# A Macaron block on one core: score products that read 32 rows of the array, layer norms scaled on VectorE, keys stored once, a shorter lead-in

## What is computed

```python
x = x + 0.5 * ffn(layernorm(x))          # sum over 8 experts: (silu(x @ Wg) * (x @ Wu)) @ Wd, inner width 512
x = x + attention(layernorm(x))          # 16 heads of 8, rotary q and k, causal, relative positions clipped to 32
x = x + 0.5 * ffn(layernorm(x))          # the same weights

scores = einsum('bhqd,bhkd->bhqk', q, k) + einsum('bhqd,qkd->bhqk', q, rel)
attn   = softmax(where(causal, scores, -1e18))
ctx    = einsum('bhqk,bhkd->bhqd', attn, v) + einsum('bhqk,qkd->bhqd', attn, rel)
```

## Time and profile before

| | us |
|---|---|
| median of three runs | 1380.19 |
| lowest and highest run | 1377.62, 1382.7 |
| profiled execution, its time | 1373.76 |
| profiled execution, span from first to last instruction | 1371.8 |

### The profile page before, as it was taken

The page is one execution under the profiler, slowest core; times in us unless marked ns, Lnnn a source line. Parts: engine busy times, 40 slices in busy tenths (PEclk is TensorE's granted clock), DMA queues, the critical chain, the costliest instruction groups (busy, mean ns, idle before and its releaser), DMA issues. The chain is left out here.

```text
span 1371.8 us, 29322 instructions
## 1 busy us (share of the span) xinstructions
PE 1333.0 (97%) x8472; PEld 1074.1 (78%) x8472; DVE 1192.4 (87%) x2554; ACT 1105.2 (81%) x2642; POOL 1098.6 (80%) x1012
## 2 busy tenths in 40 slices
PE   8999999999999999999999999999999899999798
PEld 7878777777878788778878878777888788788586
DVE  6887988998999999889899989899989889999465
ACT  6765878888888889878888888888888788888354
POOL 7977879788888888877779877889888788878465
PEclk9999999999999999999999999999999999999899
DMA  5404799999999999999999999999999989998200
GB/s 184 158 1 136 137 226 173 183 215 161 196 200 179 182 182 188 208 160 181 172 190 207 180 178 170 178 215 183 175 184 172 204 165 179 177 182 147 45 1 8
DMA packets 719138, 225.07 MB, mean 164 GB/s; under 512 B 653057, under 2 KB 698497, under 8 KB 718977
## 3 DMA queue, kind: packets, MB, share of 16 engines
q1 hardware_dynamic: 562224, 180.84, 73.4%
q10 hardware_dynamic: 156752, 42.36, 17.0%
HBM read 60.95 MB, written 69.86 MB: 95 GB/s over the span
## 5 line engine op out<-in xcount | busy, mean ns | idle before, releaser
L1231 POOL TENSOR_TENSOR hid_lo<-hid,hid_hi 128x512 fp32r<-128x512 f32 x512 | 662.1, 1302 | 149.2 <-ACT hid_hi L932 116.4
L1079 DVE TENSOR_TENSOR hid<-hid,work 128x512 f32<-128x512 f32 x512 | 347.1, 680 | 63.1 <-PE work L729 59.2
L1073 DVE SCALAR_TENSOR_TENSOR hid<-hid,work 128x512 f32<-128x512 f32 x512 | 345.2, 679 | 32.0 <-ACT hid L926 31.0
L1246 POOL TENSOR_TENSOR probs<-exps,probs 128x512 f16<-128x512 f32 (+1 forms) x288 | 307.2, 1069 | 79.0 <-ACT probs L989 76.0
L932 ACT CAST hid_hi<-hid 128x512 fp32r<-128x512 f32 x512 | 318.1, 625 | 62.0 <-DVE hid L1079 46.3
L926 ACT ACTIVATE hid<-work 128x512 f32<-128x512 f32 x512 | 307.1, 602 | 73.1 <-PE work L729 52.7
L977 ACT ACTIVATE exps<-work,negmax_shifted 128x512 f32<-128x512 f32 (+2 forms) x320 | 193.0, 605 | 40.9 <-DVE negmax_shifted L1179 25.4
L1173 DVE TENSOR_REDUCE negmax<-work 128x1 f32<-128x384 f32 (+3 forms) x352 | 222.2, 633 | 1.8
L727 PE MATMUL work<-xt,wg 128*128 128x512 f32 x512 | 205.3, 401 | 3.4 <-DVE xt L1048 1.5
L810 PE MATMUL acc<-hid_lo,wd 128*128 128x512 f32 x512 | 205.8, 405 | 0.8 <-POOL hid_lo L1231 0.7
L727 PE MATMUL work<-xt,wu 128*128 128x512 f32 x512 | 204.2, 399 | 1.0 <-DVE hid L1073 0.4
(11 more groups left out here) (99 smaller groups left out, 1909.2 us busy)
## 6 DMA issues: line engine op xcount, KB each, us to landing
prob_window_scratch<-probs SPq DMA_DIRECT2D x384, 80.0 KB, 3.0
rel_win<-rel_window_scratch ACTq DMA_DIRECT2D x250, 96.0 KB, 3.5
q_scratch<-rope SPq DMA_DIRECT2D x16, 512.0 KB, 4.7
qq<-q_scratch ACTq DMA_DIRECT2D x32, 256.0 KB
k_scratch<-rope SPq DMA_DIRECT2D x16, 512.0 KB, 3.9
rel_window_scratch<-g_s SPq DMA_DIRECT2D x32, 256.0 KB, 3.0
k_pad<-k_scratch SPq DMA_DIRECT2D x128, 64.0 KB, 3.1
prob_window_scratch<-probs SPq DMA_DIRECT2D x32, 256.0 KB, 4.8
```

What stands on the lines that cost most here:

```text
L1073: dve.scalar_tensor_tensor(out=hid[:, arg % HB, :], in0=hid[:, arg % HB, :], scalar=1.0, in1=work[bank_of["gate", arg]][:, :], op0=ALU.add ...
L1079: dve.tensor_tensor(hid[:, arg % HB, :], hid[:, arg % HB, :], work[bank_of["up", arg]][:, :], ALU.mult).then_inc(s_hid, 1)
L1231: pool.tensor_tensor(hid_lo[:, arg % HH, :], hid[:, arg % HB, :], hid_hi[:, arg % HH, :].bitcast(F32), ALU.subtract).then_inc(s_hlo, 1)
L1246: pool.tensor_tensor(probs[:, arg % PB, cols:2 * cols], exp_of(arg)[:, 0:cols], probs[:, arg % PB, 0:cols], ALU.subtract).then_inc(s_plent, 1)
```

## The change

Four things change.

1. The `scores` of tiles 2 and 3 read only the 32 rows of `qq` and `k_pad` in which their head stands. The built program gives these 256 matmuls an array shape of 32 rows by 128 columns, at row 0, 32, 64 or 96; before, all `scores` had the shape 128 by 128. In the planner, the second task of a pair (`a` odd) takes 0.02 and is due at once, and the first takes 0.19 more than before.
2. `ln_scaled` moves from ScalarE to VectorE, as `(x - mean) * rstd`; GpSimd no longer makes `mean_neg` and `shift`.
3. k is stored in two copies, not four, and `load_k` reads each twice.
4. The lead-in has 14 transposes of the identity instead of 24. A pass's first `gate` multiplies with `x_hi` twice before it waits for `x_lo`, and the wait of `project_v` on the k store is out of the planner.

The due times (`LATER`, all numbers in it, and `UNITS_TO`) are others too.

```diff
-    UNITS_FROM, UNITS_TO = 146, 1406
+    UNITS_FROM, UNITS_TO = 146, 1394
...
-    LATER = {"acc": -121.4, "attention_sum": -318.4, "band_turn": -1036.1, "band_values": -446.9, "constants":
+    LATER = {"acc": -586.1, "attention_sum": -763.3, "band_turn": -795.8, "band_values": 49.4, "constants":
...
-        step("PE", 0.683, at, "gate", n, ("gated", back(n, 2)), split[0], *normed)
+        step("PE", 0.683, at, "gate", n, ("gated", back(n, 2)), split[0], *normed, ordered=rest)
...
-        step("POOL", 1.85, time, "ln_rstd", what, ("ln_stats", what))
-        step("ACT", 1.55, time, "ln_scaled", what, ("ln_rstd", what))
+        step("POOL", 1.3, time, "ln_rstd", what, ("ln_stats", what))
+        step("DVE", 0.75, time, "ln_scaled", what, ("ln_rstd", what))
...
-            step("PE", 0.02 + columns / 2286, due[k], "scores", k, ("load_q", quad // NT),
-                 ("load_k", quad // NT), done_with(back(k, 2)))
+            beside = HEADS[i] == 1 and a % 2 == 1
+            step("PE", 0.02 if beside else 0.02 + columns / 2286 + 0.19 * (HEADS[i] == 1), -1000 if beside else due[k],
+                 "scores", k, ("load_q", quad // NT), ("load_k", quad // NT), done_with(back(k, 2)))
...
-                    for copy in range(2):
-                        sp.dma_start(bass.AP((q_t, k_t)[i], base + copy * (1 + i) * P * L,
-                                             [[L, P], [(2 - i) * P * L, 2], [1, L]]),
-                                     rope[:, :, :]).then_inc(s_qst[i], 16)
+                    if i == 0:
+                        for copy in range(2):
+                            sp.dma_start(bass.AP(q_t, (t % VB * 4 + copy) * P * L, [[L, P], [2 * P * L, 2], [1, L]]),
+                                         rope[:, :, :]).then_inc(s_qst[0], 16)
+                    else:
+                        sp.dma_start(bass.AP(k_t, t % VB * 2 * P * L, [[L, P], [P * L, 2], [1, L]]),
+                                     rope[:, :, :]).then_inc(s_qst[1], 16)
...
-            for i in range(24):
+            for i in range(14):
                 done = pe.transpose(work[0][:, 0:P], ident[:, :], ident[:, :])
...
+                    pe.matmul(bank[:, :], wg[:, HI, e, cols], x_hi, start=True, stop=False)
+                    pe.matmul(bank[:, :], wg[:, LO, e, cols], x_hi, start=False, stop=False)
+                    if k == 0:
                         pe.wait_ge(s_xlo, LN["ln1" if kind == "A" else "ln3", t] + 1)
-                    bank = take_bank(name, arg)
-                    three(bank[:, :], wg[:, HI, e, cols], wg[:, LO, e, cols],
-                          x_hi, x_lo).then_inc(s_gate, 1)
+                    pe.matmul(bank[:, :], wg[:, HI, e, cols], x_lo, start=False, stop=True).then_inc(s_gate, 1)
...
-                    pe.matmul(bank[:, 0:len(places) * keys], qq[:, gg % 2, i * P:(i + 1) * P],
-                              k_pad[:, gg % 2, places[0]:places[-1] + 1, 0:keys],
+                    rows = slice(0, P) if len(places) > 1 else slice(R * places[0], R * places[0] + R)
+                    pe.matmul(bank[:, 0:len(places) * keys], qq[rows, gg % 2, i * P:(i + 1) * P],
+                              k_pad[rows, gg % 2, places[0]:places[-1] + 1, 0:keys],
                               start=True, stop=True).then_inc(s_sc, 1)
...
+            def norm_scaled(m, x, sums):
+                dve.wait_ge(s_rstd, m + 1)
+                wait(dve, s_xnt, m)
+                wait(dve, s_ftok, sums)
+                for i in range(NT):
+                    done = dve.tensor_scalar(xn[:, i * P:(i + 1) * P], x[:, i * P:(i + 1) * P], moments[:, i, 0:1],
+                                             rstd[:, i:i + 1], ALU.subtract, ALU.mult)
+                done.then_inc(s_xn, 1)
```

More of the change, by code:

```diff
@@ L103, in macaron_kernel @@
     LANDS = {"PE": 0.35, "ACT": 0.35, "DVE": 0.35, "POOL": 0.35, "SP": 2.6}
-    LATER = {"acc": -121.4, "attention_sum": -318.4, "band_turn": -1036.1, "band_values": -446.9, "constants":
-             -30.0, "down": 8.6, "down_lo": -201.5, "exp": 12.1, "fill": 1556.9, "gate": -44.0, "gated": 320.8, "hi": 3.0,
-             "largest": -216.4, "ln_hi": -7.5, "ln_lo": -70.0, "ln_rstd": 143.1, "ln_scaled": -27.0, "ln_stats": -82.5,
-             "ln_turned": -567.8, "lo": -140.6, "load_band": -538.1, "load_expert": -1404.6, "load_k": 925.9, "load_q":
-             8.6, "load_window": 12.9, "load_x": -367.9, "near": -197.6, "outproj": -318.4, "p_hi": -260.7, "p_lent":
-             -464.6, "p_lo": -295.1, "p_turn": -31.8, "prepare_hi": 633.1, "prepare_lo": -582.6, "product": 22.2,
-             "project": -628.0, "project_v": -251.4, "qk_hi": -662.7, "qk_lo": -982.2, "qk_store": -200.1, "qrel": 5.7,
-             "qrel_copy": -216.1, "qrel_store": -370.4, "recip": -1364.0, "recip_copy": -97.4, "recip_turned": -69.4,
-             "recip_wide": 306.1, "rotate": 670.1, "scale": -238.4, "scores": -342.4, "shift": -259.0, "split_hi": 409.2,
-             "split_lo": 142.9, "store": -956.4, "store_band": -1287.5, "sum": -1014.5, "sum_turned": -630.3, "tanh": -2.0,
-             "up": 0.9, "v_add": 219.3, "v_split": -42.6, "values": -864.8, "zero": 229.9}
@@ L119, in step @@
-    def step(engine, takes, time, name, arg, *after, lands=None):
-        before = ()
+    LATER = {"acc": -586.1, "attention_sum": -763.3, "band_turn": -795.8, "band_values": 49.4, "constants":
+             1562.7, "down": 36.2, "down_lo": 4.5, "exp": 22.5, "fill": 1007.1, "gate": 25.3, "gated": 41.8, "hi": 11.9,
+             "largest": -320.0, "ln_hi": -291.6, "ln_lo": -276.9, "ln_rstd": 547.2, "ln_scaled": 288.9, "ln_stats": -792.4,
+             "ln_turned": -33.9, "lo": -501.5, "load_band": -1429.9, "load_expert": -1522.6, "load_k": 106.2, "load_q":
+             -417.2, "load_window": 166.5, "load_x": -242.0, "near": 52.1, "outproj": -124.1, "p_hi": -556.7, "p_lent":
+             -546.4, "p_lo": -852.2, "p_turn": -27.3, "prepare_hi": 176.2, "prepare_lo": 600.1, "product": -245.7,
+             "project": -80.0, "project_v": 46.4, "qk_hi": -596.3, "qk_lo": -1272.1, "qk_store": 166.5, "qrel": 36.1,
+             "qrel_copy": -7.1, "qrel_store": -451.1, "recip": -864.4, "recip_copy": 134.5, "recip_turned": 31.0,
+             "recip_wide": 347.3, "rotate": 581.4, "scale": -677.2, "scores": 8.5, "shift": -492.5, "split_hi": -441.4,
+             "split_lo": -175.9, "store": 455.7, "store_band": -1215.8, "sum": -855.8, "sum_turned": -411.0, "tanh":
+             -408.2, "up": 26.9, "v_add": 419.0, "v_split": -263.7, "values": -273.2, "zero": 1378.1}
@@ L121, in step @@
+    def step(engine, takes, time, name, arg, *after, lands=None, ordered=()):
+        before = []
         if name in ("p_lo", "p_lent", "shift"):
@@ L127, in step @@
         steps[name, arg] = (engine, takes, LANDS[engine] if lands is None else lands, time + LATER.get(name, 0.0),
-                            [what for what in after if what[1] is not None], [what for what in before if what in steps])
+                            [what for what in after if what[1] is not None],
+                            [what for what in before if what in steps] + list(ordered))
     PARTS = {"split_hi": 3, "split_lo": 3, "project": 4, "rotate": 4, "qk_hi": 2, "qk_lo": 2, "qk_store": 2}
@@ L180, in macaron_kernel @@
         kind, t = PASSES[p]
-        normed = [("ln_lo", ("ln1" if kind == "A" else "ln3", t))] if k == 0 and p else []
+        normed = [("ln_hi", ("ln1" if kind == "A" else "ln3", t))] if k == 0 and p else []
+        rest = [("ln_lo", ("ln1" if kind == "A" else "ln3", t))] if k == 0 and p else []
         split = [("split_lo", (k // FC, piece)) if p == 0 and k % FC == 0 and k else ("", None) for piece in range(3)]
-        step("PE", 0.683, at, "gate", n, ("gated", back(n, 2)), split[0], *normed)
+        step("PE", 0.683, at, "gate", n, ("gated", back(n, 2)), split[0], *normed, ordered=rest)
         step("ACT", 0.488, at + 0.9, "tanh", n, ("gate", n), ("lo", back(n, HB)))
         step("DVE", wide(L), at + 1.5, "gated", n, ("tanh", n))
-        step("PE", 0.683, at + 1, "up", n, ("product", back(n, 2)), split[1], *normed)
+        step("PE", 0.683, at + 1, "up", n, ("product", back(n, 2)), split[1], *rest)
         step("DVE", wide(L), at + 2.3, "product", n, ("gated", n), ("up", n))
@@ L438, in macaron_kernel @@
         rstd = sb("rstd", [P, NT])
-        shift = sb("shift", [P, NT])
-        mean_neg = sb("mean_neg", [P, NT])
-        zeros = sb("zeros", [P, NT])
         minus_half = sb("minus_half", [P, NT])
```

37 lines of the change are left out of this document (12 added, 25 removed).

## The result

The changed kernel takes 1619.72 us (median of 4 runs, 1619.55 to 1619.89), the kernel before 1378.9 (median of 4, 1375.93 to 1382.7). The ratio is 1.1745, with a 95% interval of 1.1714 to 1.1776. The forecast was slower, by 61 us to 1441; it is slower by 241. The direction is right and the size is far off, well outside the range.

A forecast was written before the change was run, and what follows sets the result against it. The prediction took TensorE's stream of closely packed matmuls as the bound. It summed 79 - 2 - 6 - 10 = +61 us onto 1380.2, forecasting 1441 us, with an 8-in-10 range of 1362 to 1458.

The forecast's parts named there:

- the price of an excursion: TensorE: each switch to the 32-row shape and back loses 0.37 us (0.34 to 0.40).
- The term: TensorE's scores: 233 excursions cost 86 us, less 2.5 beside `values` and 4.6 for real pairs: +79 us.
- Waits close up, 10: TensorE's idle time, 20.0 us in the long stretch: half of it goes, 10 us gained.
- SP's queue loses eight issues: Key stores: eight of 16 go, loads stay hidden, cost nothing; up to 3 us could come back.
- the norm: Four VectorE operations at 0.21 us, 0.85 us per norm, 20 us over 24 norms, covered except at the two ends.
- the cover's loss: Norms on VectorE: if other chunks no longer covered them, 20 us (33 at 0.341) would be paid.
- the lead-in, -2: Kernel start: fewer transposes and a shorter norm bring the first `gate` 2.9 us earlier, of which 2 are counted.
- the end, -6: Gap between the last two passes: earlier `band_values` and `outproj`, shorter norm and earlier `gate` save 5.4, rounded to 6 us.
- Worse, 0.07: Rival, chance 0.07: VectorE's 20 to 33 us come onto the path, or lone scores hold banks longer; 1459 to 1480.

The follow-up runs named there:

- e2: The kernel before with the 32-row score products alone: 1454.32 us, ratio 1.0570.
- e11: The changed kernel in its own order, all scores over 128 rows, k loads of 16 rows, norm operations that also write an accumulated column: 1383.35 us.
- e13: The changed kernel, 32-row scores kept, with k loads of 16 rows and norm operations that also write an accumulated column: 1455.00 us.
- e6: The kernel before, its order untouched, with only the norm's scaling moved to VectorE: 1409.52 us, ratio 1.0233.
- e10: e6 with norm operations that also write an accumulated column to a spare tile: 1384.34 us, ratio 1.0059.
- e12: The kernel before in its own order, with only the 14 lead-in transposes and the later wait in a pass's first gate: 1374.51 us, ratio 0.9993.
- e1: The changed kernel, its order untouched, with all score products over 128 rows: 1537.12 us, ratio 1.1176.
- e14: e1 with only the k loads mended, cut to 16 rows each: 1419.39 us, ratio 1.0313.
- e7: The code of the kernel before, run in the order that e3's planner gives: 1476.99 us, ratio 1.0742.
- e8: The changed kernel's code without the 32-row shape, in the order of the kernel before: 1477.30 us, ratio 1.0742.
- e3: The changed kernel with full-row scores, and the duration of scores and the table LATER as before: 1577.12 us, ratio 1.1461.

## Why the prediction was wrong, and where it was right

**Right: the price of an excursion and how it counts.** The term was 86 - 2.5 - 4.6 = 79 us gross. One excursion measured 0.41 us (forecast 0.37, bounds 0.34 to 0.40), pairs run side by side and pay once, and singles gain nothing from streaming beside anything. Three comparisons give 79, 80 and 70 us net. At 0.40 the 233 excursions make 93, less 7 for pairs and neighbours of `values`, 86, of which 7 to 16 us didn't show. "Waits close up, 10" is near: TensorE's idle time fell by 4 us in e2 and by 8 from e11 to e13. That the term's 79 is met so exactly is luck in part: it takes a clean excursion too small (0.37), counts all at that price where e2 shows many to be cheaper, and stands before the waits are taken off.

**Wrong: "SP's queue loses eight issues. Its cover is whatever hides the loads now, so I cost it at nothing."** This is the step that failed, by 119 us. I counted bytes and issues of the edit and didn't read its address list. It measured +93 alone, and 119 in the changed order is what the loads of 16 rows give back. The cover was real for a load whose packets start within 4 us; but the transposes of `probs_t` stand behind the load in the same queue, `bands` and `rel_win` use the same engines, and with two engines held for twice the time, those behind it are late. How much of it is the queue and how much the engines wasn't separated. The earlier trace rows already named `probs_t` as the longest wait of all: that was the wait with no slack to give.

**Wrong: the norm, "I take 0.21: 0.85 us per norm ... covered by other chunks except at the two ends".** The size was off: 0.68 to 0.71 us per operation (e6 and the changed kernel) where I took 0.21, bounded by 0.341. The bound came from a single operation that met an idle GpSimd, and is right for that case: e6's took 0.336 then. But GpSimd is busy 80% of the span, so the meeting is the normal case. And the cover failed: 33 and 35 us are on the path, not nothing. Most of that is the wait for GpSimd, for e10 keeps VectorE longer than I had assumed (0.40 us and 0.08 for its second instruction) and costs 8. The remark that the cover's loss would cost 20 to 33 us was right in size by chance, since it counts 0.21 to 0.341 us of work per operation and no wait.

**Wrong with it: the lead-in, -2.** The transposes started at 9.56, not near 6.8, because the norm's four operations took 3.10 us beside GpSimd's splits; the first `gate` came 0.33 us sooner in place of 2.9. Alone, the edit measured nothing (e12).

**Right: the end, -6.** The gap between the last two passes went from 12.98 to 6.46 us. No run has this edit alone, so its 6 us of the total are read from the gap and not from a time.

**Not priced at all: the long waits' second cost.** Behind the gap of 6 us shown above TensorE is granted 1.2 GHz for a stretch. In the whole trace it runs at this level for 176 us, in 29 stretches, where before it was 33 us in 7; the mean clock of the runs fell from 0.989 to about 0.948. The k loads show what this is worth: e1 and e14 stream the same matmuls, e14's profiled span is 113.5 us shorter, and of that TensorE's idle time gives 78 and its busy time 35 (1384.1 to 1348.9), at a granted clock of 0.955 and 0.980. So about a third of that loss was no wait, but matmuls at the lower clock behind the waits.

**The rivals.** "Worse, 0.07" named VectorE's term on the path and banks held longer, 1459 to 1480. Its first half happened, at the bound's upper end; but no rival had a transfer that slows its neighbours. Something else that I believed on the way, and that fell: that the new order is bad. e7 (+100) seemed to show it, and e8 with e1 left 61 us for it. But e11 is at +7. The 61 us were late loads and norms that cost more in the new order (119 against 76 and 35 against 24); that it gives them less room is my reading and wasn't measured. What makes e3's order, which is another, cost 100 us with before's code stays open.

## What to carry to other kernels

Read an edited transfer's address list and not only its bytes: ask what its outermost dimension is, and price it by what waits behind it in the same queue, not by what waits for it. Price an operation that is moved to an engine by its spread in the trace and by what the engine next to it does at that moment, not by one short row. When several small edits come together and the sum is far off, mend each suspect in the new order as well as trying it in the old one, for a cost can grow there and look like the order's own.

## What the runs showed of the hardware

- Four loads with a repeated read as their outermost dimension of 2 started their 128 packets of 84 ns over 6.7 us (median); with 32 outermost over 2.6, with 16 in eight loads over 4.1. In before's order 69 of 352 transposing DMAs then took over 2.5 us to issue in place of 24, and `bands`, on another queue, landed after 9.7 us in place of 5.0 (in the changed order 12.8, and 7.3 in e14 with loads of 16).
- A two-scalar operation on VectorE of 128x128 fp32 took 332 ns at best and 336 on average with GpSimd idle, and up to 1401 ns beside it, ending 0.05 to 0.1 us behind GpSimd's operation in most cases; with an accumulated output it took 394 to 410 ns, always, and 83 for a second instruction.
- A lone 32-row product among full-size ones costs 0.40 to 0.41 us: about 0.09 before it, 0.20 (0.09 and 0.11) behind it, and 0.11 in front of the matmul after the next. It is the sum that the column strips of `values` had let me expect, with one weight load more.
